# A fused two-layer decoder on one core: the prologue rearranged, and the orders of its steps with it

## What is computed

```python
dt = clip(exp(log_dt), 1e-4, 1)
log_A = log(clip(exp(-exp(A_log) * dt[:, None]), 1e-8, 1 - 1e-8))      # 128 x 16
A_mean = exp(t_idx[:, None, None] * log_A[None]).mean(axis=1)          # 256 x 16: mean over the 128 channels
x_mean = causal_convolution(B_proj, A_mean)                            # per state, along the sequence
y = ((x_mean @ W_C.T + D_skip * x_proj) * silu(z)) @ W_out.T + b_out
x = x + y + layernorm(x)       # the block's own residual is the normalised x
```

## Time and profile before

| | us |
|---|---|
| median of 3 runs (727.42 to 731.83) | 729.11 |
| the profiled execution's span | 728.7 |
| PE busy in it | 634.2 |
| DVE busy | 550.5 |
| ACT busy | 438.1 |
| POOL busy | 178.4 |

### The profile page before, as it was taken

How to read it: one execution, slowest core, us unless ns; L and a number is a source line. 1 busy time by engine, 2 the same in 40 slices (tenths; PEclk the granted TensorE clock), 3 DMA queues, 4 the chain that set the end, 5 groups by cost and what they waited for, 6 DMA issues and landing times.

```text
span 728.7 us, 14858 instructions
## 1 busy us (share of the span) xinstructions
PE 634.2 (87%) x5800; PEld 430.9 (59%) x5800; DVE 550.5 (76%) x1513; ACT 438.1 (60%) x863; POOL 178.4 (24%) x348
## 2 busy tenths in 40 slices
PE   2688899899799998899888997978999899999887
PEld 0255458458556685558645684554567467674556
DVE  7559986858987789776878468899758965777783
ACT  4124666675676646756577544756775678767534
POOL 9614411102132222211241033051132102020202
PEclk9989999999999999999999999999999999999999
DMA  8400000000000000000000000000000000000000
GB/s 298 119 2 9 1 1 1 2 1 1 1 22 2 2 9 7 9 1 1 16 2 1 1 2 15 2 1 1 2 16 2 1 1 1 1 1 2 2 1 22
DMA packets 10358, 10.62 MB, mean 15 GB/s; under 512 B 2832, under 2 KB 9520, under 8 KB 10032
## 3 DMA queue, kind: packets, MB, share of 16 engines
q1 hardware_dynamic: 9568, 6.98, 3.3%
q10 hardware_dynamic: 720, 2.69, 0.9%
HBM read 8.60 MB, written 1.07 MB: 13 GB/s over the span
## 4 chain that ended last, share of the span: by engine, by line
PE 49%; DVE 32%; ACT 11%; issue 4%; POOL 2%; DMA 1%; ACTq 1%; SPq 0%; POOLq 0%; DVEq 0%
DVE qs L1150 8%; PE psA L1562 8%; PE psB L1549 8%; PE psO L1500 6%; ACT P L839 5%; PE psB L1476 4%; PE psA L1460 4%; PE psM L1439 4%; DVE QT L1138 4%; DVE qs L1145 3%; PE psM L1358 3%; PE psM L1315 2%; ACT QT L836 2%; DVE stats L948 1%; DVE kz_s L1131 1%
## 5 line engine op out<-in xcount | busy, mean ns | idle before, releaser
L839 ACT ACTIVATE P<-psB 128x512 f32<-128x512 f32 x320 | 176.9, 597 | 71.5 <-PE psB L1476 46.1
L1150 DVE TENSOR_REDUCE qs<-psA 128x2 bf16<-128x512 f32 x256 | 165.4, 690 | 26.6 <-PE psA L1460 25.4
L1460 PE MATMUL psA<-kz_s,QT 128*128 128x512 bf16 x256 | 90.7, 385 | 13.7 <-DVE qs L1150 8.0
L1476 PE MATMUL psB<-QT,kz_s 128*128 128x256 bf16 x512 | 90.6, 276 | 9.7 <-ACT QT L836 3.2
L846 ACT ACTIVATE P<-psB,W 128x256 f32<-128x256 f32 x160 | 66.4, 473 | 39.8 <-PE psB L1549 34.8
L1439 PE MATMUL psM<-identb,qs 128*128 128x128 bf16 x896 | 72.4, 222 | 11.0 <-DVE qs L1145 2.9
L1439 PEld LDWEIGHTS psM<-identb,qs 128*128 128x128 bf16 x896 | 56.3, 99 | 31.6 <-issue 8.0
L1500 PE MATMUL psO<-P,vp 128*32 128x256 f32 x1024 | 68.3, 385 | 2.1 <-ACT P L839 1.5
L1476 PEld LDWEIGHTS psB<-QT,kz_s 128*128 128x128 bf16 x512 | 39.2, 98 | 52.2 <-ACT P L839 26.3
L1562 PE MATMUL psA<-w,P 128*128 128x128 f32 x512 | 66.1, 277 | 1.8 <-ACT P L846 0.9
L661 POOL TENSOR_SCALAR veps<-mv 128x2 f32<-128x2 f32 x40 | 10.4, 261 | 229.2 <-DVE mv L952 228.6
(11 more groups left out here) (178 smaller groups left out, 1109.8 us busy)
## 6 DMA issues: line engine op xcount, KB each, us to landing
w<-expert_w ACTq DMA_DIRECT2D x2, 1024.0 KB, 10.3
toep<-decay_rows SPq DMA_DIRECT2D x4, 512.0 KB, 5.9
x<-x SPq DMA_DIRECT2D x8, 128.0 KB, 2.8
y<-base SPq DMA_DIRECT2D x8, 128.0 KB, 1.9
W<-weights SPq DMA_DIRECT2D x1, 940.0 KB, 6.9
rows<-bias_rows SPq DMA_DIRECT2D x1, 872.0 KB, 10.4
ctxp<-context SPq DMA_DIRECT2D x8, 64.0 KB, 2.1
fw<-mlp_w ACTq DMA_DIRECT2D x2, 256.0 KB, 10.9
```

Source lines behind the costliest of these rows:

```text
L839: act.activation(P[:, p, :, :].rearrange("p a s -> p (a s)"), psB[:, s.u % B_BANKS, :], ACT.Exp, scale=LAYERS[s.L]["scale"]).then_inc(b_dr ...
L1150: dve.tensor_reduce(qs[L["W"]][j][:, t * H + h:t * H + h + 2, 0], ps.rearrange("p (h c) -> p h c", h=2), AX.X, ALU.max, negate=True).then_ ...
L1460: ins = pe.matmul(ps, QT[j][:, h // L["HB"], t * 128:t * 128 + 128], kz[s.L][j][:, kv:kv + 2, :].rearrange("p h s -> p (h s)"), start=True ...
L1476: ins = pe.matmul(ps[:, i * S:i * S + S], kz[s.L][j][:, kv + i, kc * 128:kc * 128 + 128], QT[j][:, h // L["HB"], :], start=True, stop=True)
```

## The change

- **Means.** A stationary operand of two columns, `pick`, sends two states to row 0 and two to row 1 of one bank; two matmuls accumulate in a bank, so that four banks (two of `psB`, two of `psA`) hold all 16 rows. PE waits for no copy. DVE copies four 2x512 blocks.
- **Rows to DRAM and back.** Each of the four blocks is stored, and read back as four states of `toep`, as soon as it is there, instead of all after the last.
- **Loads.** ACT starts the main parts of `weights` and `bias_rows`, `wc` and `rope` at its very beginning, then a dummy exponential; the expert and MLP weights are loaded by SP after the Toeplitz blocks. SP keeps the early parts, x and the context.
- **Blanks and presets.** DVE zeroes the query buffers and the small key buffer first, the large key buffers between the copies and after the first T3. POOL presets the context buffers' rest after the first three T1, and the slots' buffers after the first T6.
- **Centring** moves behind the first T1 on PE, into two `psO` banks, and its copies behind the second T2 on ACT.
- **ORDER** is rewritten: on PE 658 of 1304 steps stand at another place, on DVE 253 of 736, on ACT 133 of 664, on POOL 65 of 120, most by one to three places, spread over the whole program.

```diff
-        "00w001010010w101000a10a1a021aawaaa1011010101b0wbb2bb0bb0000b001a001001a001aa10a0ax0aaa00aa10aa1aa1ba1a211aa1a1"
...
+        "0w0101010w100010000a1aa10201aawaaa1011010b0110wbb2bb00bb00a0b001001001a100a1a00aax0aaa01aa00aa1a2a1a1ab11aa1a1"
...
-            sp.dma_start(W[:, early_w:W_N], w_in[:, early_w:W_N]).then_inc(weights_loaded, 16)
-            sp.dma_start(rows[:, early_r:R_N], rows_in[early_r:R_N].partition_broadcast(128)).then_inc(weights_loaded, 16)
-            sp.dma_start(rope[:, :], rope_in).then_inc(weights_loaded, 16)
-            sp.dma_start(wc[:, :], wc_in).then_inc(weights_loaded, 16)
             load_context(0)
...
-            sp.wait_ge(decay_row, NS // 2)
-            sp.dma_start(decay[:, 0:S].unsqueeze(0), P[0:1, 0:NS // 2, :, :].rearrange("p a b s -> p (a b) s")).then_inc(decay_stored, 16)
-            sp.wait_ge(decay_stored, 32)
-            for n in range(4):
...
+            def keep_rows(n):
+
+                sp.wait_ge(decay_row, n + 1)
+                sp.dma_start(decay[4 * n:4 * n + 4, 0:S].rearrange("(p a) s -> p a s", a=2), P[0:2, n, :, :]).then_inc(rows_kept[n], 16)
...
+            keep_rows(0)
+            for n in range(4):
+                if n < 3:
+                    keep_rows(n + 1)
+                spread_rows(n)
+            sp.dma_start(w1[:, :], w1_in).then_inc(weights2_loaded, 16)
...
+            contexts_made = slots_made = False
             for s in order["POOL"]:
                 j = s.j
+                if not contexts_made and s.kind != "T1":
+                    preset_contexts()
+                    contexts_made = True
+                if not slots_made and s.kind not in ("T1", "C", "T6"):
+                    preset_slots()
+                    slots_made = True
...
+            act.dma_start(W[:, early_w:W_N], w_in[:, early_w:W_N]).then_inc(weights_loaded, 16)
+            act.dma_start(rows[:, early_r:R_N], rows_in[early_r:R_N].partition_broadcast(128)).then_inc(weights_loaded, 16)
...
+            act.activation(dt[:, 4:5], zero[:, :], ACT.Exp).then_inc(table_warm, 1)
             if ahead(early_loaded, 32):
                 act.wait_ge(early_loaded, 32)
-            act.dma_start(w1[:, :], w1_in).then_inc(weights2_loaded, 16)
...
-                for n in range(NS // 2):
+                for n in range(4):
                     if ahead(decay_mean, n + 1):
                         dve.wait_ge(decay_mean, n + 1)
-                    dve.tensor_copy(P[0:1, n, :, :].rearrange("p a s -> p (a s)"), psB[0:1, n % 2, :]).then_inc(decay_row, 1)
+                    dve.tensor_copy(P[0:2, n, :, :].rearrange("p a s -> p (a s)"), mean_bank(n)[0:2, :]).then_inc(decay_row, 1)
+                    if n < 3:
+                        blank(kz["s0"][n // 2], H // 2 * (n % 2), H // 2 * (n % 2) + H // 2)
...
-                if n >= 2:
-                    if ahead(decay_row, n - 1):
-                        pe.wait_ge(decay_row, n - 1)
-                pe.matmul(psB[0:1, n % 2, :], wc_("ones")[:, 0:1], toep[:, 2 * n:2 * n + 2, :].rearrange("p a s -> p (a s)"),
-                          start=True, stop=True).then_inc(decay_mean, 1)
-            if ahead(decay_row, NS // 2):
-                pe.wait_ge(decay_row, NS // 2)
+            for n in range(4):
+                for k in range(2):
+                    if ahead(decay_terms, 4 * n + 2 * k + 4):
+                        pe.wait_ge(decay_terms, 4 * n + 2 * k + 4)
+                    ins = pe.matmul(mean_bank(n)[0:2, :], pick[:, 2 * k:2 * k + 2],
+                                    toep[:, 4 * n + 2 * k:4 * n + 2 * k + 2, :].rearrange("p a s -> p (a s)"), start=(k == 0), stop=(k == 1))
+                ins.then_inc(decay_mean, 1)
```

More of the change, by code:

```diff
@@ L599, in _, with preset_contexts @@
                     preset(t[:, :, :], 0.0)
-            for j in range(SLOTS):
-                for t in (ks["s0"][j], ks["s1"][j], on4[j]):
+            def preset_contexts():
+                for t in (kx["x0"], kx["x1"]):
                     preset(t[:, :, :], 0.0)
[L603 to L607, removed]
@@ L609, in _ @@
-            for j in range(SLOTS):
-                for t in (ks["s0"][j], ks["s1"][j]):
+                if ahead(presets_done, presets[0]):
+                    pool.wait_ge(presets_done, presets[0])
+                for t in (kx["x0"], kx["x1"]):
                     preset(t[:, :, 0:MS], 1.0)
                 for half in range(2):
-                    preset(value_view(vp[j], 4, half, DEN, DEN + 1), 1.0)
-            for t in (kx["x0"], kx["x1"]):
-                preset(t[:, :, 0:MS], 1.0)
@@ L617, in _ @@
                 if ahead(presets_done, presets[0]):
                     pool.wait_ge(presets_done, presets[0])
[L619 to L624, removed]
             done = [0]
@@ L780, in claim @@
                 return s.p
+            centred = False
             for s in order["ACT"]:
                 j = s.j
+                if not centred and s.kind not in ("T1", "T2"):
+                    take_centred()
+                    centred = True
+                if s.L != "m":
+                    blanks = SLOTS if s.L == "x0" else BLANKS
+                    if ahead(blocks_blank, blanks):
+                        act.wait_ge(blocks_blank, blanks)
                 if s.kind in ("T1", "P1"):
@@ L914, in store_rows, with blank_rest, prepared @@
                 dve.tensor_scalar(W[:, cx + 448:cx + 640], W[:, cx + 448:cx + 640], wc_("rmsg"), None, ALU.mult).then_inc(gains_in, 1)
-            def prepared(value):
+            def blank_rest():
+                for n in range(3, 2 * SLOTS):
+                    blank(kz["s0"][n // 2], H // 2 * (n % 2), H // 2 * (n % 2) + H // 2)
+            def prepared(s):
+                value = 2 if s.kind == "T3" else context_presets[0] if s.kind == "C" or s.L == "x0" else presets[0]
                 if ahead(presets_done, value):
                     dve.wait_ge(presets_done, value)
-                if ahead(blocks_blank, 3 * SLOTS):
-                    dve.wait_ge(blocks_blank, 3 * SLOTS)
+                if s.kind not in ("T3", "C"):
+                    blanks = SLOTS if s.L == "x0" else BLANKS
+                    if ahead(blocks_blank, blanks):
+                        dve.wait_ge(blocks_blank, blanks)
             done = [0]
@@ L965, in _ @@
                     rows_stored = True
+                if not all_blank and s.kind not in ("T1", "T3", "C"):
+                    blank_rest()
+                    all_blank = True
                 if s.L != "m":
-                    prepared(presets[0])
+                    prepared(s)
                 if s.kind in ("T1", "P1"):
@@ L1287, in take, with prepared @@
+            def prepared(s):
+                value = context_presets[0] if s.kind == "C" or s.L == "x0" else presets[0]
+                if ahead(presets_done, value):
+                    pe.wait_ge(presets_done, value)
+                if s.kind != "C":
+                    blanks = SLOTS if s.L == "x0" else BLANKS
+                    if ahead(blocks_blank, blanks):
+                        pe.wait_ge(blocks_blank, blanks)
             def take(s):
```

182 lines of the change are left out of this document (110 added, 72 removed).

## The result

| | us |
|---|---|
| before, median of 5 runs (727.42 to 731.83) | 729.18 |
| changed, median of 5 runs (716.53 to 719.68) | 718.9 |
| ratio, 95% interval | 0.9832 (0.9809 to 0.9855) |
| span of the profiled execution, before and changed | 728.7, 714.7 |

The ratio times 729.1 is 716.9, a gain of 12.2 us where 6.8 was forecast, and just beyond the range, which ended at 717.8. The two medians alone lie 10.3 us apart, and 718.9 would be just inside. Measured again beside other kernels, the changed kernel had a ratio of 0.9842 (0.9806 to 0.9878), 11.5 us. So the direction was right and the size too small by a third to nearly a half. The profiled execution is the fastest of the five, so its own 14.0 flatters the change by about 2.

What follows compares the result with a forecast made beforehand. After about 60 us PE's steps and small waits set the time; before that, a single prologue chain. A lead of 5.8 at the second x plus 1.0 at the end took 6.8 off 728.7: 721.9, or 722.3 against the median; range 717.8 to 729.5.

Steps and rivals of the forecast that it cites:

- (a): Loads and start: with ACT starting the main loads, the first exponential comes 1.7 us earlier.
- X: Start of the first of the 16 exponentials, forecast at 9.4 us, where it was 11.13.
- (b): Means: 16 passes on PE without a wait for copies take 9.5 us, winning a further 3.3 us.
- K: End of the last copy of the rows of means, forecast at 20.5 us, where it was 25.55.
- (c): From K to the first T4: 7.85 us instead of 9.16, a gain of 1.3, T4 starting at 28.35.
- (d): First T4 to first new x: both T4 at full clock, x at 37.7 against 42.17, 4.5 us earlier.
- (e): First to second new x: some 1.3 us of DVE's wait goes; lead 5.8, x at 49.1 against 54.88.
- rival A: PE stays at the lower clock level at the front: 725.8 or 726.6 us; chance 0.16.
- (f): End of the kernel: F1 of sequence 7 comes ahead of a normalisation on DVE, 1.0 us won.
- The rest of the order: Moved steps elsewhere, 658 of 1304 places on PE: 0 net, with 2 to 4 us either way.
- B: Rival: the loop gives the lead back through 16 net new waits, 729.1 us, no change; chance 0.19.
- C: Rival: the loop costs more, from 24 net new waits the kernel is slower, 733 us and above; chance 0.08.

Runs made afterwards that it cites:

- loads_on_sp: Changed kernel with the main loads of weights and rows, wc and rope started by SP again, behind early parts, x and context; ratio 0.9817.
- h_oldorder: Changed prologue with the orders of the kernel before throughout, on all four engines; ratio 0.9970, 2.2 us.
- h_front: Changed prologue with the new orders for the first 60 us or so only, the orders of before from there; ratio 0.9929, 5.2 us.
- one_place: As h_front, but with the new order also at one place near 305 to 316 us (33 PE, 15 DVE, 19 ACT steps); ratio 0.9932.
- warm: Changed kernel plus 16 matmuls on zeroed data on PE before its wait for the early loads, and 2 more later; ratio 0.9831.

## Why the prediction was right or wrong, step by step

- **(a) Loads: right sum by luck, wrong bound.** X was 9.89 (9.4 forecast, 7.8 to 10.0). The early rows landed at 8.29, beyond the 7.6 that I took for the latest, since I had looked at the 940 KB alone; DVE needed 1.6 and not 2.4 after them, and the two misses partly cancel. loads_on_sp shows that moving the loads to ACT delays the early rows by 4.0. By the Trainium skill ("DMA: Bandwidth & Descriptors", "Issuing engines are not separate DMA queues"), loads started by different engines run on the same DMA engines and interleave; the delay agrees with that, and the landing came later still than the 7.6 that I had worked out from it. What the part won is that ACT is ready at the landing: X follows it by 1.6 us and no longer by 6.4; 3.5 of these 4.8 went into the later landing.
- **(b) Means: right.** The passes took 8.5 to 10.0 us (9.5 forecast), and K stood at 20.1 to 21.6 (20.5). Their number at the slow rate varies, as bounded.
- **(c), (d) To the first T4 and the x: right, (c) 0.9 too long.** T4 began at 27.0 to 28.6 in six executions with this prologue and these front orders (28.35 forecast), always 6.9 behind K (7.85). Both T4 took 2.81 at the higher level (2.74), and x(0) stood at 36.3 to 37.8 (37.7). In h_oldorder, where PE stands idle for 3.49 ahead of it, T4 takes 5.22.
- **(e) Second x: right in its sum**, 48.5 to 50.3 (49.1). But of the 1.3 us that were to be won between the first x and the second, 0.2 to 0.5 came: PE waits 3.94 for the split queries there and is at half clock from 41.15 to 47.97. So the 0.9 us by which (c) was too long and the 0.8 to 1.1 by which (e) won less cancel. POOL's presets ended at 37.89 (38). Of the lead 1.6 is lost soon after, by 78 us; some 1.1 of it is a stretch at half clock from 68.45, which the second execution of the same kernel does not have. So rival A was right that PE would not keep the level, only later than where it looked.
- **(f) Tail: right**, 1.1 (1.0), 0.6 of it from the swap.
- **The rest of the order: here it failed.** "I take 0 net, with 2 to 4 us either way": it was 5.2, where the front, forecast at 5.8, came out at 5.2 too (h_front). The step priced one kind of wait, PE's scores behind DVE's maxima, at 0.43 each, and gave the chances of a loss (B and C, 0.27) far more weight than those of a gain (D, 0.04, at 4 us). That wait stayed as it was, 28.0 and 28.3 us. What went were small idle stretches of PE on other steps, as the copies of QT in one_place: 3.05 us of 19.18 in the stretch that was compared, up to 320 us. For the rest of the loop it is not shown which waits went. The prediction counted the moved steps and did not lay any of them on the gaps of the old trace, where at least this place could be read: the kernel before waits the same 0.68, 0.44 and 0.28 us there, at 316.48, 321.24 and 323.03.

## What to carry to other kernels

In this in-order loop, whose PE is busy 87% of the span, a lead won at the front lasted to the end nearly unchanged (3.7 to 3.4 us), so front and loop could be priced apart and added. A reordering need not be noise around zero: lay the moved steps on the gaps in the old trace, one by one, and sum those that a moved step now fills. Do not start a large load from another engine ahead of the small one that the program waits for: here it cost 4.0 us of landing.

## What the runs showed of the hardware

- PE's first passes run at half speed, and the column of the granted clock says 1.00 there. In the changed kernel:

```profile
10.94:14.35 3.41, 3.41 (x5) 0.56 (x6) 1.47 (x14) 3.41 (x10) 2.17 (x6) 1.00 0.00 0
```

  Five records fall into these 3.41 us, up to the fourth pass each 0.80 to 0.86 from the next, against 0.43 later; in warm, where PE had worked before, 0.43 from the first. The trace has no record of the clock at all ahead of 13.84, where the passes get faster (ahead of 16.64 in h_front, with more slow passes), so 1.00 stands for a missing record there. In the words of the Trainium skill ("TensorE: Matmul & The Clock Gate", Part 1, "What's actually happening"), "the default state is throttled, and activity releases the throttle"; the pace of the passes agrees.
- A stretch at PE's lower level cost between 0.6 us (from 489.07 in the kernel before) and 1.7 (a T4 of 4.49 against 2.81), and comes at other places in other executions of the same kernel. The changed kernel has one from 68.45 in its first execution and none there in its second, which has one from 434.76 instead; they cost 1.1 and 1.0. That is a third of the 3 us between the runs of this kernel.
